# GpSimd sums the derived token quarters from quarters that DMA has turned; the next x is prepared one step earlier

## The chip, the cores and the metric

One core of one Trainium2 chip. The metric is device time per execution in microseconds (us); lower is better. Three runs of the kernel before gave a median of 3518.05 us (3515.58 to 3518.43).

## The reference

The input x has 8 x 1024 tokens of 512 features. The kernel computes `x + s * g`, where `xn = layernorm(x)`, `s` is an attention block of 16 heads on `xn`, and `g = silu(spikes(y) / 5)` with

```python
h = square(relu(xn @ W_fc.T))        # 512 -> 2048
y = h @ W_proj.T                     # 2048 -> 512
# five steps of a leaky integrator count how often it passes its threshold
```

The change concerns how `xn @ W_fc.T` gets its moving operands. The kernel does that product by a Strassen-like scheme: a block of 512 tokens by 512 features is cut into quarters (two halves of the tokens by two halves of the features), and seven products of quarters or of sums of quarters take the place of eight. Every operand is split into a high and a low f16 part, and three of the four partial products are kept.

## The kernel before, in words

The first stage is the feed-forward block, on 16 chunks (`NC` = 16, `c` = 0 to 15) of 512 tokens. A chunk has 8 steps (`PAIRS` = 8, `p` = 0 to 7, `n = 8c + p`). In a step TensorE does the seven products of one slice of 256 hidden features (`product(n, 0)` to `product(n, 6)`, six matmuls each, L727), and between them eight groups of projection matmuls for the hidden slices of earlier steps (`proj`, L744). The second stage, attention, begins at about 1376 us; only its first group of heads is prepared inside the last two chunks.

All engines run a fixed order that is written out by hand (`step` in each engine's block); semaphores keep them together. In each step:

- ACT copies partial sums out of PSUM (`snapshot` 0 to 2, L982, and `take_sum`, L988) and makes the high parts of the hidden slices (`hid_hi`, L975). `after_first` to `after_fourth` are the places for other work; `after_fourth` comes behind `take_sum`. ACT also issues the load of the next weights (L890).
- VectorE adds the partial sums (`combine(n, 0)` to `combine(n, 2)`, L1335; product 3 waits for `combine` 0, product 6 for `combine` 1, product 1 of the next step for `combine` 2), squares (`square`, L1320) and makes low parts (`hid_lo`, L1327). In steps 2 to 5 it counts the spikes of the chunk before (`count`, L168 and L171), in steps 4, 6 and 7 it makes gate tiles (`gate_tile`, L178).
- GpSimd multiplies each gate tile by gamma and adds beta's part to x (`multiply`, L123, L125, L127: three instructions for each of four tiles).

While chunk c runs, chunk c + 1 is prepared. For c of 1 or more: VectorE takes statistics of x in step 0 (`statistics`, L1229; `variances`), normalises in step 1 (L1261), ACT and VectorE split into high and low f16 in steps 2 and 3 (`part_hi`, L925; `part_lo`, L1277). SP then issues 32 DMAs that turn 128x128 pieces of it (`turn`, L496: two parts, four tiles of tokens, four blocks of features) into `xnT`: these are the natural quarters, with the features on the partitions. For chunk 1, in chunk 0, all this is one step later.

The four derived quarters are made apart from that. GpSimd forms them on the unturned `xn` (`make_turns`, L587 to L592, four instructions of 128x512), into the memory in which x had stood; ACT and VectorE split them (`turned_hi`, L931, in steps 3 and 4; `turned_lo`, L1281, in steps 4 and 5); TensorE turns them through PSUM (`turn_quarter`, L638, four groups of eight matmuls in two steps named by `TURN_AT`, steps 5 and 6); ACT copies them out (`copy_turned`, L941) into `xnS`. When the derived quarters have been split, ACT issues the load of the following x (`fetch_x`, L946). For chunk 0 other functions do this.

SP's queue within chunk c: store `xnT` of chunk c to memory, load x again for the output (`load_base`), copy rows of a table, issue the 32 turns for chunk c + 1, and at last, when GpSimd has done the twelve multiplications of chunk c - 1, store gate and base (L160).

## Time and profile before

| | us |
|---|---|
| median of three runs | 3518.05 |
| the profiled execution | 3518.49 |
| its span, first to last instruction | 3516.7 |
| TensorE busy | 3384.6 |
| VectorE busy | 2804.3 |
| ACT busy | 2779.1 |
| GpSimd busy | 1862.4 |
| feed-forward stage, 27.5 to about 1376 | 1349 |
| a regular chunk of it (531.23 to 612.29) | 81.06 |

PE is TensorE, DVE is VectorE, POOL is GpSimd, SP the engine that issues most DMAs. Busy times are unions over the span; `x` counts instructions. PEclk is the granted TensorE clock as a share of 2.4 GHz. A chunk's times below are counted from its first product, steps from their own.

### The profile page before, as it was taken

The page shows a single profiled execution, that of the slowest core. Times are in us where ns is not written, and L with a number is a line of the kernel's source. Part 1 is how long each engine was busy: PE and PEld are TensorE (multiplying, and loading weights), DVE is VectorE, ACT ScalarE, POOL GpSimd, SP SyncE. Part 2 cuts the span into 40 slices and gives each one's busy share as a digit, 9 for nine tenths or more (in the row PEclk, how much of TensorE's full clock was granted, in tenths as well). Part 3 has the DMA queues.
Part 4 walks back from the last instruction along what each step waited for, and adds up shares of the span by engine and source line. Part 5 has one row for each costly group of instructions (what it writes and reads, how often), then busy time and mean ns, then how long its engine had stood idle before and what let it go on. Part 6 is the DMA issues. An engine that isn't in the chain of part 4 may idle for free.

```text
span 3516.7 us, 63651 instructions
## 1 busy us (share of the span) xinstructions
PE 3384.6 (96%) x22764; PEld 1693.4 (48%) x22764; DVE 2804.3 (80%) x4812; ACT 2779.1 (79%) x4531; POOL 1862.4 (53%) x1094
## 2 busy tenths in 40 slices
PE   6999999999999999999999999999999999999996
PEld 4666666666666665334334334433433433433432
DVE  7878887777877866777788788788788888888887
ACT  6555444444444455999999999999999999999996
POOL 4223332223222314998756766766766766666662
PEclk9999999999999999999999999999999999999998
DMA  5655555555555543222332232232332322322322
GB/s 204 210 165 177 196 173 180 189 190 176 168 176 175 166 150 119 72 67 82 112 100 79 88 94 81 92 94 81 92 94 80 93 91 82 94 88 82 98 61 85
DMA packets 257226, 430.34 MB, mean 122 GB/s; under 512 B 98672, under 2 KB 134256, under 8 KB 256912
## 3 DMA queue, kind: packets, MB, share of 16 engines
q1 hardware_dynamic: 231088, 294.13, 27.1%
q10 hardware_dynamic: 25824, 132.13, 10.8%
q8 instruction: 183, 3.00, 0.4%
q14 instruction: 131, 1.07, 0.1%
HBM read 284.75 MB, written 83.95 MB: 105 GB/s over the span
## 4 chain that ended last, share of the span: by engine, by line
ACT 32%; PE 13%; issue 10%; DVE 4%; SPq 1%; DMA 1%; ACTq 0%; DVEq 0%
ACT recurrence_or_probs L1903 17%; ACT s_sb L1910 15%; PE misc L1777 3%; PE acc L1852 3%; PE s_ps L1832 3%; PE s_ps L1818 3%; DVE s_sb L1979 2%; SPq L320 1%; DMA xT<-xnT 1%; DVE gate_or_tokens L2108 1%; PE misc L1759 0%; DVE x_or_queries L2016 0%; DVE outT L1999 0%; DVE gate_or_tokens L2111 0%; PE s_ps L1777 0%
## 5 line engine op out<-in xcount | busy, mean ns | idle before, releaser
L1979 DVE TENSOR_SCALAR_CACHE_REDUCE s_sb<-s_ps 128x1024 f32<-128x1024 f32 x998 | 1214.4, 1221 | 354.4 <-PE s_ps L1818 326.3
L2185 POOL TENSOR_TENSOR recurrence_or_probs<-recurrence_or_probs,toep 128x512 f32<-128x512 f32 (+1 forms) x375 | 1288.9, 3458 | 365.9 <-ACT recurrence_or_probs L1903 365.5
L1910 ACT ACTIVATE s_sb<-s_sb,nmax 128x1024 f32<-128x1024 f32 x998 | 1166.3, 1169 | 9.7 <-DVE s_sb L1979 9.2
L1903 ACT ACTIVATE recurrence_or_probs<-s_ps 128x1024 f32<-128x1024 f32 x1024 | 1060.5, 1037 | 9.5 <-PE s_ps L1832 9.3
L744 PE MATMUL ps_y<-w_pr,hid_part 128*128 128x512 f16 x3072 | 807.6, 379 | 0.0
L1852 PE MATMUL acc<-recurrence_or_probs,val 128*32 128x512 f32 x4096 | 546.6, 606 | 2.2 <-DVE recurrence_or_probs L2095 1.5
L982 ACT ACTIVATE snap<-ps_fc 128x256 f32<-128x256 f32 x384 | 147.5, 384 | 468.7 <-PE ps_fc L727 453.7
L123 POOL TENSOR_TENSOR recurrence_or_probs<-gate_or_tokens,gamma_beta 128x512 f32<-128x512 f32 x60 | 86.0, 1434 | 595.5 <-DVE gate_or_tokens L178 594.4
L744 PEld LDWEIGHTS ps_y<-w_pr,hid_part 128*128 128x128 f16 x3072 | 300.5, 98 | 173.4
L727 PE MATMUL ps_fc<-xnT_part,w_fc 128*128 128x256 f16 x2304 | 314.8, 273 | 17.8 <-DVE u L1335 11.6
L1818 PE MATMUL s_ps<-kst,qst 96*128 96x512 f16 x1024 | 306.0, 380 | 25.5 <-ACT recurrence_or_probs L1903 25.4
L1832 PE MATMUL s_ps<-x_or_queries 99*128 99x512 f16 x1024 | 307.5, 381 | 5.3 <-DVE s_sb L1979 5.2
L1832 PE MATMUL s_ps<-qst,kst 99*128 99x512 f16 x1024 | 307.7, 383 | 1.7 <-DVE s_sb L1979 1.6
L1818 PE MATMUL s_ps<-x_or_queries 96*128 96x512 f16 x972 | 290.3, 379 | 15.8 <-ACT recurrence_or_probs L1903 15.8
L727 PEld LDWEIGHTS ps_fc<-xnT_part,w_fc 128*128 128x128 f16 x2304 | 222.2, 98 | 124.3 <-DVE u L1335 20.3
L1320 DVE SCALAR_TENSOR_TENSOR hid<-u 128x512 f32<-128x512 f32 x256 | 202.5, 791 | 97.7 <-ACT u L988 49.1
L1335 DVE TENSOR_TENSOR u<-ps_fc,snap 128x256 f32<-128x256 f32 x384 | 161.2, 420 | 143.4 <-PE ps_fc L727 77.3
L1327 DVE TENSOR_TENSOR hid_part<-hid,hid_part 128x512 f16<-128x512 f32 x256 | 238.3, 934 | 11.9 <-ACT hid_part L975 11.8
L1910 ACT ACTIVATION_READ_ACCUMULATOR s_sb<-s_sb,nmax 128x1 f32 x998 | 219.4, 220 | 0.0
L727 PE MATMUL ps_fc<-xnS_part,w_fc 128*128 128x256 f16 x1536 | 210.2, 273 | 9.1 <-DVE u L1335 6.8
L727 PE MATMUL ps_fc<-recurrence_or_probs,w_fc 128*128 128x256 f16 x1536 | 209.6, 273 | 3.8 <-DVE u L1335 3.0
L171 DVE SCALAR_TENSOR_TENSOR recurrence_or_probs<-recurrence_or_probs 128x512 f32<-128x512 f32 x240 | 190.8, 795 | 0.6
(206 smaller groups left out, 4076.9 us busy)
## 6 DMA issues: line engine op xcount, KB each, us to landing
w_fc<-fc_made ACTq DMA_DIRECT2D x120, 896.0 KB, 5.0
toep<-table_rows SPq DMA_DIRECT2D x32, 2048.0 KB, 8.3
x_or_queries<-x_or_queries SPq DMA_DIRECT2D x384, 64.0 KB, 2.0
xnT<-xnT_part SPq DMA_DIRECT2D x32, 512.0 KB, 11.3
x_or_gate<-in_x SPq DMA_DIRECT2D x16, 1024.0 KB, 9.1
...
```

The lines of the kernel that those rows point to most:

```text
L171: op = self.nc.vector.scalar_tensor_tensor(spikes, y, self.thresholds[i], spikes, ALU.is_ge, ALU.add)
L727: last = nc.tensor.matmul(bank, w["fc"][:, n % RINGW, i, a, k, :], moving, start=(m == 0 and i in (0, 1, 3)), stop=(m == 5), skip_group_ch ...
L744: last = nc.tensor.matmul(ps_y[:, t, :], hid_part[:, f % 4, a, t * P:(t + 1) * P], w["pr"][:, b, f, :], start=(f == 0 and m == 0), stop=(f ...
L1320: nc.vector.scalar_tensor_tensor(hid[:, f, :], u[:, f, :], 0.0, u[:, f, :], ALU.max, ALU.mult).then_inc(sq_done, 1)
L1327: nc.vector.tensor_tensor(hid_part[:, f % 4, 1, :], hid[:, f % 2, :], hid_part[:, f % 4, 0, :], ALU.subtract).then_inc(lo_done, 1)
L1818: last = nc.tensor.matmul(s_ps[:, item_buffer(x), c * 512:(c + 1) * 512], qst[par][0:ROWS, j, st * P:(st + 1) * P], kst[par][0:ROWS, j, c ...
L1832: last = nc.tensor.matmul(s_ps[:, item_buffer(x), i * 512:(i + 1) * 512], kst[s.par][:ROWS + SUBTRACTED, j, tb * P:(tb + 1) * P], qst[s.pa ...
L1852: last = nc.tensor.matmul(acc[j * HD:(j + 1) * HD, :], val[:, par, tb, j * HD:(j + 1) * HD], prob[:, k % PROBS, j, :], start=(tb == 0), st ...
L1903: nc.scalar.activation(prob[:, k % PROBS, 2 * second:2 * second + 2, :].rearrange("p j n -> p (j n)"), s_ps[:, item_buffer(pair_item(m)), ...
L1910: nc.scalar.activation(s_sb[:, i % 4, :], s_sb[:, i % 4, :], ACT.Exp, bias=nmax[:, par, j, st:st + 1], scale=-1.0, accum_out=den[:, par, j ...
L1979: nc.vector.tensor_scalar(s_sb[:, i % 4, :], s_ps[:, item_buffer(tile_item(n)), :], -1.0, None, ALU.mult, ALU.min, accum_out=nmax[:, par, ...
L2185: nc.gpsimd.tensor_tensor(tile, tile, toep[:, par, :, at:at + width], ALU.add).then_inc(biased, 1)
```

## The change

For chunks 2 to 15, GpSimd makes the derived quarters from the turned natural quarters: `join_quarter` adds the high and the low part of a natural quarter in `xnT` (f16) into `xn` (f32, whose normalised values are no longer needed then), and `turned_sum` forms a difference or sum of two of these. ACT and VectorE split the results straight into `xnS` (`turned_hi`, `turned_lo`). `make_turns`, `turn_quarter` and `copy_turned` remain for chunk 1 alone (and chunk 0 as before). SP issues the 32 turns by quarters, in the order of need, each quarter after both of its parts are split, and counts each quarter on a semaphore of its own. The splitting of the derived quarters stands in steps 5, 6 and 7 of a chunk (6 and 7 in chunk 1). The preparation of x (`prepared`) begins in step 7 of the chunk before from chunk 3's x on, one step sooner; the load of x moves from ACT to SP, ahead of the turns. In steps 23, 30 and 31 the four `qkv_lo` are spread otherwise over the step.

```diff
@@ -207,15 +207,15 @@
-TURN_AT = {c * 8 + 5 + (c == 0) + h: (c + 1, 2 * h) for c in range(15) for h in range(2)}
+TURN_AT = {6: (1, 0), 7: (1, 2)}
...
-TURNS_AT = ({4: (0, 1), 5: (2, 3)}, {3: (0, 1), 4: (2, 3)})
-TURNS_LO_AT = ({5: (0, 1), 6: (2, 3)}, {4: (0, 1), 5: (2, 3)})
+TURNS_AT = ({4: (0, 1), 5: (2, 3)}, {6: (0, 1), 7: (2, 3)}, {5: (0,), 6: (1, 2), 7: (3,)})
+TURNS_LO_AT = ({5: (0, 1), 6: (2, 3)}, {6: (0, 1), 7: (2, 3)}, {5: (0,), 6: (1, 2), 7: (3,)})
...
@@ -468,6 +469,27 @@
+        def prepared(n, k):
+            n -= k
+            if n == 1:
+                return 1
+            if n == PAIRS:
+                return 2
+            c = (n + 1) // PAIRS + 1
+            return c if n > PAIRS and n % PAIRS == PAIRS - 1 and c < NC else None
+        def wait_turned(eng, c):
+            if c > 0:
+                for q in range(4):
+                    eng.wait_ge(xt_turned[q], c * TURNED)
+        def natural(par, part, q):
+            k, half = ((2, HALF), (0, 0), (0, HALF), (2, 0))[q]
+            return xnT[:, par, part, k:k + 2, half:half + HALF]
...
@@ -489,12 +511,14 @@
-                for part, done in ((0, xn_hi), (1, xn_lo)):
-                    for t in range(4):
-                        sp.wait_ge(done, (c - 1) * 4 + t + 1)
-                        for k in range(EB):
-                            sp.dma_start(xnT[:, par, part, k, t * P:(t + 1) * P], xn_part[:, part, t, k * P:(k + 1) * P],
-                                         transpose=True).then_inc(xt_turned, 16)
+                for q, tokens_half, k_half in ((2, 1, 0), (0, 1, 1), (1, 0, 0), (3, 0, 1)):
+                    sp.wait_ge(xn_hi, c * 4 - 2 + 2 * tokens_half)
+                    sp.wait_ge(xn_lo, c * 4 - 2 + 2 * tokens_half)
+                    for part in range(2):
+                        for t in (2 * tokens_half, 2 * tokens_half + 1):
+                            for k in (2 * k_half, 2 * k_half + 1):
+                                sp.dma_start(xnT[:, par, part, k, t * P:(t + 1) * P], xn_part[:, part, t, k * P:(k + 1) * P],
+                                             transpose=True).then_inc(xt_turned[q], 16)
...
@@ -531,6 +555,9 @@
+                if 0 < c < NC - 2:
+                    sp.wait_ge(xn_ready, c * 4 + 8)
+                    load_x(c + 2)
...
@@ -542,8 +569,9 @@
-                    sp.wait_ge(xt_turned, (NC - 1) * TURNED)
-                    sp.wait_ge(xs_ps, NC * 4)
+                    wait_turned(sp, NC - 1)
+                    sp.wait_ge(turn_hi, (NC - 1) * 4)
+                    sp.wait_ge(turn_lo, (NC - 1) * 4)
...
@@ -590,6 +618,20 @@
+            def join_quarter(c, q, done):
+                if done == 0:
+                    pool.wait_ge(xn_hi, c * 4)
+                    pool.wait_ge(xn_lo, c * 4)
+                pool.wait_ge(xt_turned[q], c * TURNED)
+                nc.gpsimd.tensor_tensor(xn[:, q, :].rearrange("p (k s) -> p k s", k=2), natural(c % 2, 0, q), natural(c % 2, 1, q),
+                                        ALU.add).then_inc(sum_made, 1)
+            def turned_sum(c, q, a, b, op, done):
+                pool.wait_ge(sum_made, (c - 2) * 8 + done)
+                nc.gpsimd.tensor_tensor(xn[:, q, :], xn[:, a, :], xn[:, b, :], op).then_inc(sum_made, 1)
...
@@ -606,17 +648,25 @@
-            for c in range(1, NC):
-                if c < NC - 1:
-                    make_turns(c + 1)
-                else:
-                    pool.wait_ge(xt_turned, (NC - 1) * TURNED)
-                    nc.gpsimd.memset(first.kst[ROWS:ROWS + SUBTRACTED], 1.0).then_inc(first.ones_set, 1)
-                    pool.wait_ge(first.ones_set, 1)
-                for t in range(4):
+            for c in range(1, NC - 1):
+                join_quarter(c + 1, 2, 0)
+                join_quarter(c + 1, 0, 1)
+                turned_sum(c + 1, 0, 0, 2, ALU.subtract, 2)
+                spiking.multiply(c - 1, 0)
+                join_quarter(c + 1, 1, 3)
+                turned_sum(c + 1, 2, 2, 1, ALU.subtract, 4)
+                turned_sum(c + 1, 1, 0, 1, ALU.add, 5)
+                join_quarter(c + 1, 3, 6)
+                turned_sum(c + 1, 3, 3, 1, ALU.subtract, 7)
+                for t in range(1, 4):
...
-                    if c == NC - 1 and t == 0:
-                        first.subtracted(pool, 0, 0, 0)
+            wait_turned(pool, NC - 1)
+            nc.gpsimd.memset(first.kst[ROWS:ROWS + SUBTRACTED], 1.0).then_inc(first.ones_set, 1)
+            pool.wait_ge(first.ones_set, 1)
+            for t in range(4):
+                spiking.multiply(NC - 2, t)
+                if t == 0:
+                    first.subtracted(pool, 0, 0, 0)
...
@@ -716,6 +766,10 @@
+                if n > PAIRS and p == 0 and i in (2, 3, 4, 6):
+                    made = (c - 1) * 4 + {2: 2, 3: 2, 4: 3, 6: 4}[i]
+                    pe.wait_ge(turn_hi, made)
+                    pe.wait_ge(turn_lo, made)
...
@@ -921,14 +975,20 @@
-                    wait(act, xt_turned, (c - 1) * TURNED)
+                    wait_turned(act, c - 1)
...
-                if j == 0:
-                    act.wait_ge(turns_made, c * 4 + 4)
-                    act.wait_ge(xn_lo, c * 4)
-                nc.scalar.activation(turn_part[:, 0, j], turns[:, j], ACT.Copy).then_inc(turn_hi, 1)
+                if c == 1:
+                    if j == 0:
+                        act.wait_ge(turns_made, c * 4 + 4)
+                        act.wait_ge(xn_lo, c * 4)
+                    nc.scalar.activation(turn_part[:, 0, j], turns[:, j], ACT.Copy).then_inc(turn_hi, 1)
+                else:
+                    if j == 0:
+                        act.wait_ge(multiplied, (c - 1) * PAIRS * PRODUCTS)
+                    act.wait_ge(sum_made, (c - 2) * 8 + (3, 6, 6, 8)[j])
+                    nc.scalar.activation(xnS[c % 2][:, 0, j].rearrange("p k s -> p (k s)"), xn[:, j, :], ACT.Copy).then_inc(turn_hi, 1)
...
@@ -1074,8 +1125,8 @@
-                if c < NC - 1 and p in TURNS_AT[c > 0]:
-                    for j in TURNS_AT[c > 0][p]:
+                if c < NC - 1 and p in TURNS_AT[min(c, 2)]:
+                    for j in TURNS_AT[min(c, 2)][p]:
...
@@ -1257,7 +1308,11 @@
-                    wait(dve, xs_ps, c * 4)
+                    if c <= 2:
+                        wait(dve, xs_ps, c * 4)
+                    else:
+                        dve.wait_ge(turn_hi, (c - 1) * 4)
+                        dve.wait_ge(turn_lo, (c - 1) * 4)
...
@@ -1273,12 +1328,16 @@
-                    wait(dve, xt_turned, (c - 1) * TURNED)
+                    wait_turned(dve, c - 1)
...
-                nc.vector.tensor_tensor(turn_part[:, 1, j], turns[:, j], turn_part[:, 0, j], ALU.subtract).then_inc(turn_lo, 1)
+                if c == 1:
+                    nc.vector.tensor_tensor(turn_part[:, 1, j], turns[:, j], turn_part[:, 0, j], ALU.subtract).then_inc(turn_lo, 1)
+                else:
+                    hi, lo = (xnS[c % 2][:, part, j].rearrange("p k s -> p (k s)") for part in range(2))
+                    nc.vector.tensor_tensor(lo, xn[:, j, :], hi, ALU.subtract).then_inc(turn_lo, 1)
...
@@ -1344,14 +1403,15 @@
-                ahead, late = c < NC - 1, c == 0
+                ahead = c < NC - 1
+                begun, refined, split = prepared(n, 0), prepared(n, 1), (prepared(n, 2), prepared(n, 3))
...
-                if ahead and p == 0 + late:
-                    statistics(c + 1, 0)
+                if begun:
+                    statistics(begun, 0)
...
-                if ahead and p == 3 + late:
-                    part_lo(c + 1, 2)
+                if split[1]:
+                    part_lo(split[1], 2)
...
@@ -1360,45 +1420,48 @@
-                if ahead and p == 0 + late:
+                if n in QKV_LO_AT:
+                    qkv_lo(QKV_LO_AT[n], 0)
+                if begun:
...
-                        statistics(c + 1, t)
-                if ahead and p == 1 + late:
-                    refine(c + 1)
-                    normalise(c + 1, 0)
-                    normalise(c + 1, 1)
+                        statistics(begun, t)
+                if refined:
+                    refine(refined)
+                    normalise(refined, 0)
+                    normalise(refined, 1)
...
-                if ahead and p == 2 + late:
-                    part_lo(c + 1, 0)
-                if ahead and p == 3 + late:
-                    part_lo(c + 1, 3)
+                if split[0]:
+                    part_lo(split[0], 0)
+                if split[1]:
+                    part_lo(split[1], 3)
...
-                    for k in range(3):
-                        qkv_lo(QKV_LO_AT[n], k)
+                    qkv_lo(QKV_LO_AT[n], 1)
...
+                if n in QKV_LO_AT:
+                    qkv_lo(QKV_LO_AT[n], 2)
...
-                if ahead and p == 1 + late:
-                    normalise(c + 1, 2)
+                if refined:
+                    normalise(refined, 2)
...
-                if ahead and p == 0 + late:
-                    variances(c + 1)
+                if begun:
+                    variances(begun)
...
-                if ahead and p == 1 + late:
-                    normalise(c + 1, 3)
+                if refined:
+                    normalise(refined, 3)
...
-                if ahead and p == 2 + late:
-                    part_lo(c + 1, 1)
-                if ahead and p in TURNS_LO_AT[c > 0]:
-                    for j in TURNS_LO_AT[c > 0][p]:
+                if split[0]:
+                    part_lo(split[0], 1)
+                if ahead and p in TURNS_LO_AT[min(c, 2)]:
+                    for j in TURNS_LO_AT[min(c, 2)][p]:
...
...
```

## Rows read from the trace of the kernel before

**Rows 1.** Page, part 1: busy us, share of the span, instructions, by engine.

```profile
PE 3384.6 (96%) x22764; PEld 1693.4 (48%) x22764; DVE 2804.3 (80%) x4812; ACT 2779.1 (79%) x4531; POOL 1862.4 (53%) x1094
```

**Rows 2.** Windows of chunk 6, whole and steps 2, 4, 5, 6: stretch, length, then busy us.

```profile
531.23:612.29 81.06, 80.25 (x561) 53.29 (x560) 63.78 (x106) 38.37 (x82) 24.02 (x16) 1.00 0.53 177
...
550.76:560.52 9.76, 9.76 (x67) 6.45 (x66) 9.74 (x14) 4.76 (x10) 3.78 (x3) 1.00 0.35 109
...
570.28:580.31 10.03, 9.93 (x67) 6.38 (x66) 8.89 (x12) 5.28 (x11) 4.75 (x3) 1.00 0.41 116
...
580.31:591.85 11.54, 10.84 (x83) 7.27 (x82) 10.03 (x18) 6.20 (x13) 0.00 (x0) 1.00 0.36 105
...
591.85:602.51 10.66, 10.66 (x83) 7.35 (x82) 5.82 (x10) 6.19 (x13) 6.40 (x5) 1.00 0.60 198
```

**Rows 3.** Timeline of TensorE, step 3 of chunk 6: start, duration, instructions merged.

```profile
560.53 0.71 PE L727 MATMUL ps_fc<-xnT_part,w_fc 128*128 128x256 f16 x5
...
568.99 0.82 PE L727 MATMUL ps_fc<-xnS_part,w_fc 128*128 128x256 f16 x6
...
571.60 0.27 PE L727 MATMUL ps_fc<-xnT_part,w_fc 128*128 128x256 f16 x1
```

**Rows 4.** Timeline of TensorE, step 5 of chunk 6, with the wait before it.

```profile
582.50 0.83 PE L727 MATMUL ps_fc<-xnT_part,w_fc 128*128 128x256 f16 x6 [0.70 <-DVE u L1335]
...
583.82 0.61 PE L638 MATMUL ps_t<-identh,x_or_queries 128*128 128x128 f16 x8
...
584.26 0.27 PE L727 MATMUL ps_fc<-xnS_part,w_fc 128*128 128x256 f16 x1
```

**Rows 5.** Instructions of line 638, the turning matmuls, in the whole span.

```profile
L638 PE MATMUL ps_t<-identh,x_or_queries x480: 219/219/230, 98.4 to 1254.1; 128*128 128x128 f16 x160
```

**Rows 6.** Timeline of GpSimd, chunk 6: two of make_turns, the last multiplication.

```profile
548.57 1.27 POOL L587 TENSOR_TENSOR x_or_queries<-x_or_queries 128x512 f32<-128x512 f32 x1 [19.21 <-DVE x_or_queries L1261]
...
551.47 1.73 POOL L590 TENSOR_TENSOR x_or_queries<-x_or_queries 128x512 f32<-128x512 f32 x1
...
608.82 1.60 POOL L127 TENSOR_TENSOR gate_or_tokens<-gate_or_tokens,gamma_beta 128x512 f32<-128x512 f32 x1
```

**Rows 7.** VectorE in chunk 6: line 1327's times (ns, min/median/max), then its timeline.

```profile
L1327 DVE TENSOR_TENSOR hid_part<-hid,hid_part x16: 675/683/1754, 533.7 to 607.5; 128x512 f16<-128x512 f32 x16
...
551.99 1.50 DVE L168 TENSOR_SCALAR recurrence_or_probs<-recurrence_or_probs 128x512 f32<-128x512 f32 x1
...
559.03 0.68 DVE L1277 TENSOR_TENSOR x_or_queries<-x_or_queries 128x512 f16<-128x512 f32 x1
...
559.63 0.68 DVE L1320 SCALAR_TENSOR_TENSOR hid<-u 128x512 f32<-128x512 f32 x1
...
602.67 1.31 DVE L1320 SCALAR_TENSOR_TENSOR hid<-u 128x512 f32<-128x512 f32 x1
...
603.90 1.76 DVE L178 SCALAR_TENSOR_TENSOR gate_or_tokens<-recurrence_or_probs,gate_or_tokens 128x512 f32<-128x512 f32 x1
...
605.58 0.41 DVE L1335 TENSOR_TENSOR u<-ps_fc,snap 128x256 f32<-128x256 f32 x1
...
605.91 3.38 DVE L1327 TENSOR_TENSOR hid_part<-hid,hid_part 128x512 f16<-128x512 f32 x2
```

**Rows 8.** SP in chunk 6: the 32 turns in its timeline; all turns' time to landing.

```profile
553.29 43.61 SPq L496 DMA_TRANSPOSE xnT_part<-x_or_queries  x32
...
DMA to landing us min/median/max: 2.2/3.1/7.7
```

**Rows 9.** Timelines around chunk 1's start: SP's turns, VectorE's last split, TensorE.

```profile
65.66 45.84 SPq L496 DMA_TRANSPOSE xnT_part<-x_or_queries  x32
...
81.83 0.68 DVE L1277 TENSOR_TENSOR x_or_queries<-x_or_queries 128x512 f16<-128x512 f32 x1
...
117.12 0.82 PE L727 MATMUL ps_fc<-xnT_part,w_fc 128*128 128x256 f16 x6
```

**Rows 10.** Window behind the first product: busy us, then granted clock (PEclk).

```profile
27.46:40.00 12.54, 10.33 (x63) 6.22 (x64) 7.07 (x14) 9.82 (x14) 3.96 (x6) 0.86 0.78 288
```

**Rows 11.** Timeline of ACT, end of step 4 of chunk 6: two turned_hi.

```profile
578.59 1.14 ACT L931 ACTIVATE x_or_queries<-x_or_queries 128x512 f16<-128x512 f32 x2
```

42 lines of the change are left out of this document (17 added, 25 removed).

## The prediction

> **What bounds the kernel now.** I read the page first: TensorE is busy for 96% of the span [rows 1]. The attention stage (from about 1376 us on) is not touched by the change, so I read the feed-forward stage alone, by chunks. The windows of one regular chunk (531.23 to 612.29, number 6 of 0 to 15, one of ten alike, chunks 4 to 13) show TensorE busy for 80.25 of 81.06 us [rows 2]. The steps of it show where it is not full: an unstalled step takes 9.76 us, step 4 takes 10.03, step 5 takes 11.54, step 6 takes 10.66 and step 7 the rest, 9.78. So a chunk is 8 x 9.76 = 78.1 plus 2.95 us. The timeline of TensorE tells what the 2.95 are [rows 4]: four groups of eight turning matmuls, each of 584.26 - 583.82 = 0.44 us, 1.78 together; and waits for VectorE (L1335, the `combine`) of 2.95 - 1.78 = 1.17 us, of which the largest stands before 582.50.
>
> So TensorE bounds a regular chunk, and VectorE is a close second. Why it is late in steps 4 and 5 is seen by laying the GpSimd rows [rows 6] beside the VectorE rows [rows 7]. A subtraction of two SBUF tensors (L1327) takes 0.68 us, and 1.75 while GpSimd runs (two in 3.38 us from 605.91); the square (L1320) takes 1.31 instead of 0.68; the gate 1.76 instead of 0.68. A `combine`, which reads PSUM, stays at 0.41. GpSimd's multiplications stretch to 1.6 us too. GpSimd is idle most of a chunk (24.0 of 81 us busy, and its share by step stands in [rows 2]), so this price is paid today in few steps.
>
> When VectorE is late enough to cost something follows from a regular step of TensorE [rows 3]: product 6 starts 568.99 - 560.53 = 8.46 us into the step and needs `combine` 1; product 1 of the next step starts 11.07 us after the step's start and needs `combine` 2. Everything that VectorE finishes later than that stops TensorE.
>
> **The change, part by part.**
>
> *Turning gone.* 480 turning matmuls are 15 chunks of 32 [rows 5]; chunks 2 to 15 lose theirs, 14 x 1.78 = 24.9 us, all on the path. ACT loses eight copies per chunk; it is not the bound, worth nothing. If the 1.17 us of waits went as well in 14 chunks, 16 us more.
>
> *GpSimd.* Per chunk four `make_turns` (5.9 us, steps 1 and 2, where VectorE has room) go, and eight instructions come: four `join_quarter` and four `turned_sum`. The sums have the shape of [rows 6]. For a join of two f16 inputs there is no row: below, 1.27 us (the fp32 sum undisturbed), above, 1.73 with some conversion on top; I take 1.5, since VectorE will be busy beside it. The Trainium skill (GPSIMD Engine Reference, 3.1 Elementwise — side-by-side cycle accounting) gives about 2.6 cycles per element for two inputs and so 4497 ns for 2048 elements; by that the join would be about 1.1 us (an estimate), four of them 1.6 us less, and the sum below some 10 us lower. No run here shows which.
>
> *When the joins can run.* They wait for the DMA turns, which SP issues one after another: 32 in 43.61 us, landing 3.1 us (median) after issue, up to 7.7 [rows 8]. Today the first goes as soon as the first tile is split; in the new order it waits for all eight halves, the last of which is `part_lo` 3, now in step 2. `part_lo` is 0.68 us (559.03 in [rows 7]); its place in step 2 puts it at about 24 us from the chunk's start. At 43.61 / 4 = 10.9 us for eight turns, and two or three more for the last landing, the quarters are there at about 36, 47, 57 and 68 us. SP reaches the turns in time: after GpSimd's last multiplication it needs some 10 us for its stores and loads, the moved load of x (one issue) included. x then has four steps until step 7: hidden.
>
> GpSimd's queue, in its order: join at 36; join, difference 47 to 50; the previous chunk's `multiply` of tile 0 (three instructions) 50 to 55; join and two sums 57 to 61; join and sum 68 to 71; nine multiplications 71 to 86. From 47 to 86 it is busy for about 31 of 39 us, and that is exactly steps 5 to 7.
>
> *VectorE in steps 5 to 7.* `turned_lo` moves there (one, two, one), the statistics of the next x move into step 7 (2.4 us and 0.8 of aggregates). I lay the instructions out with the two prices of [rows 7], an instruction starting about 0.08 before the end of the last one as there.
> Step 5 (starts 48.8): square 1.3, first count 1.5, `combine` 0 at 52.1, subtraction 1.7, count 1.5, then count, subtraction free, count 1.6; `combine` 1 ends at 58.5, wanted at 57.3: 1.2 late. Count 1.7, `turned_lo` 1.5, square 0.7; `combine` 2 ends at 62.6, wanted at 61.1: 1.5 late. With undisturbed GpSimd times (1.3 each) it is 1.6 instead of 2.7.
> Step 6: GpSimd is quiet until the last quarter lands. But `turned_lo` now stands behind `turned_hi` of the same step, which ACT starts 8.3 us into it (578.59 in [rows 11], in the step from 570.28). Two of them at 1.75 under GpSimd, the square at 1.3: `combine` 2 ends 13.9 us into the step, wanted at 11.07: 2.8 late.
> Step 7: square, one statistic, gate (1.76), `combine` 0: 1.3 late; two subtractions at 1.7, three statistics, `combine` 1: 0.3 to 0.9 more. Then GpSimd ends, and step 0 is free. I take the statistics (one input) as undisturbed; no row of this stage shows them beside GpSimd, and at most they would cost as the two-input ones do, 1.07 each.
> If the third quarter lands a microsecond later, step 5 loses less and step 7, nearer to the multiplications, as much more. Sum: 6.1 to 7.9 us, I take 7.0. A chunk is then 78.1 + 7.0 = 85.1 against 81.06: +4.05, ten regular chunks +40.5.
>
> *Chunk 1* still prepares one step late, so its quarters land 10 us later (46, 57, 66, 78) while `turned_hi` for two quarters is due at the end of step 6 (67): the sums are there at about 72, ACT and with it VectorE stand for 5 us, step 7 adds 3: 86.6 against 81.07, +5.5. *Chunks 2 and 3* also carry the splitting of the attention weights in steps 6 and 7, and chunk 2 the rest of GpSimd's late work: +5 each. *Chunk 14* has 10 us of attention matmuls in steps 5 to 7, which give VectorE room: turning gone, waits come, 0 (bounds -3, +4).
>
> *The start of chunk 1.* The new issue order has its price once. Today the 32 turns for chunk 1 are issued from 65.66 to 111.50, and TensorE, which waits for the landing of all of them, begins the chunk at 117.12 [rows 9]. In the new order none starts before the last `part_lo`, at 82.5 (81.83 + 0.68). 82.6 plus 42 to 46 plus a landing is 127 to 131: TensorE stands still for 10 to 14 us, I take 12. The clock may fall as well: in the 12.54 us behind the start of the first product, before which TensorE had waited, the granted clock was 0.86, so a part of them at 1.2 instead of 2.4 GHz [rows 10]; that is (1 - 0.86) x 12.54 = 1.8 us of work, which I count inside the 10 to 14.
>
> *The rest* (the split of `qkv_lo` within its step, the new waits of SP, TensorE and DVE before the attention stage) is under work that is there anyway: 0; without that cover below 1 us each.
>
> Sum against the profiled execution (3518.49, 0.44 above the median of the runs): 12 + 5.5 + 10 + 40.5 + 0 = +68, 3586 us. The removed 24.9 us are inside the chunk differences.
>
> **Rivals.**
> A, faster: *TensorE stays the bound.* VectorE's added time fits into its slack (it is busy 63.8 of 81 us), or the joins disturb it less than fp32 sums do. What decides is `combine` 1 of step 5: done by 57.3, nothing is lost there. Then -24.9, waits between today's and none (0 to -16), +12 at chunk 1: 3489 to 3506. For: on average there is room. Against: the price is plain where both engines run, the sixteen L1327 of chunk 6 go from 0.675 to 1.754 us [rows 7], and the joins stand in three steps in a row. Chance 0.17.
> B: *it pays back what it saves.* Half of my waits come: 3.5 us per chunk in place of 2.95, so +0.5 in 13 chunks, +12, and the weights' chunks: 3526 to 3548. For: GpSimd may be less disturbed than taken. Chance 0.14; a fourth of it so low that it can't be told from no change.
> C: *the sums come too late everywhere.* If the DMA turns slip by 6 us or more (landing took up to 7.7), ACT stands before `turned_hi` in step 6 of each chunk, as it does in chunk 1. +9 in 14 chunks and 12: 3656. Against: 5.7 us of slack in step 6. Chance 0.08.
>
> **How the numbers follow.** My case has 0.61, from 3548 to 3620. About 0.2% (7 us) is what a measurement of this kernel tells from no change. Faster: A, 0.17. Same: 0.04, out of B. Slower: 0.79. The range leaves out C and the lower half of A: 3498 to 3622.
>
> **What would show it.** Right: steps 5, 6 and 7 of a regular chunk take over 11 us each with TensorE waiting for L1335; `turned_lo` at 1.75 us; GpSimd busy from 47 to 86 us of the chunk; one TensorE gap of 10 us or more near 117 us. Wrong: regular chunks of 78 to 80 us, or joins beside which VectorE keeps 0.68. Wrong in size: the quarters landing elsewhere than at 36, 47, 57 and 68.

## The result, and the profile after

The kernel after takes 3577.22 us (median of four runs, 3562.65 to 3580.01) against 3516.89 (four runs, 3515.58 to 3518.43) beside it: ratio 1.0157, interval 1.0124 to 1.0189. It is slower, by 60 us where the prediction said 68.

The page of the kernel after, the engines' busy times (us, share of the span of 3577.8 us, instructions):

```profile
PE 3384.0 (95%) x22316; PEld 1673.5 (47%) x22316; DVE 2848.3 (80%) x4812; ACT 2724.2 (76%) x4419; POOL 1943.6 (54%) x1150
```

TensorE has 448 matmuls fewer and is busy as long as before [rows 1], in a span 61.1 us longer. Two things hide in that: its waits, and matmuls that run at the lower of its two clock levels. To find where the 61 us lie I took the starts of the first product of each step from the trace; the differences are the lengths of chunks and steps.

| chunk | before | after | difference |
|---|---|---|---|
| 0 (to the first product of chunk 1) | 89.66 | 101.33 | +11.67 |
| 1 | 81.07 | 87.02 | +5.95 |
| 2 | 85.90 | 96.45 | +10.55 |
| 3 | 85.01 | 91.25 | +6.24 |
| 4 to 13, ten regular ones | 810.7 | 838.7 | +28.0 |
| 14 | 91.99 | 90.07 | -1.92 |
| 15 (to the end of its last product) | 95.06 | 95.07 | 0 |

They add up to 60.5; what follows chunk 15 is the same to 0.5 us.

**The start of chunk 1.** The timeline of TensorE in the kernel after, then its windows around the gap (length, busy us of PE, PEld, DVE, ACT, POOL, then PEclk, DMA share, GB/s):

```profile
116.79 0.59 PE L798 MATMUL ps_y<-w_pr,hid_part 128*128 128x512 f16 x2
128.88 1.44 PE L781 MATMUL ps_fc<-xnT_part,w_fc 128*128 128x256 f16 x6 [11.49 <-DMA xnT_part<-x_or_queries]
```

```profile
117.00:128.80 11.80, 0.38 (x2) 0.00 (x0) 1.49 (x3) 0.00 (x0) 0.00 (x0) 0.64 0.13 25
128.80:141.00 12.20, 12.12 (x66) 7.34 (x67) 6.65 (x17) 3.91 (x8) 0.00 (x0) 0.79 1.01 350
```

TensorE stands still for 11.49 us until the turned quarters have landed. Then six matmuls take 1.44 us instead of 0.82 [rows 9]: the granted clock is 0.79 in the next 12.2 us, so a part of them runs at 1.2 instead of 2.4 GHz, and step 0 of chunk 1 is 12.24 us long instead of 9.76.

**A regular chunk.** Chunk 6 is now 574.16 to 658.16. Its steps 4 to 7 and the whole, in the windows of the kernel after (columns as above):

```profile
613.47:623.23 9.76, 9.76 (x67) 6.44 (x66) 7.26 (x13) 4.24 (x9) 2.14 (x2) 1.00 0.40 118
623.23:632.99 9.76, 9.76 (x67) 6.47 (x66) 9.53 (x11) 4.76 (x10) 6.05 (x5) 1.00 0.39 120
632.99:644.38 11.39, 9.94 (x67) 6.38 (x66) 8.15 (x12) 5.28 (x11) 5.34 (x5) 1.00 0.35 103
644.38:658.16 13.78, 11.63 (x68) 7.02 (x66) 13.20 (x20) 3.20 (x7) 13.22 (x9) 0.88 0.20 67
574.16:658.16 84.00, 80.32 (x530) 52.05 (x528) 65.63 (x107) 34.36 (x74) 27.91 (x20) 0.98 0.52 171
```

Against [rows 2]: step 5, the longest before, is free; step 7 takes 13.78 us, with VectorE and GpSimd both busy nearly all of it. TensorE's busy time there is 11.63 us where the same matmuls take 9.76 in step 5, at a granted clock of 0.88. So the loss in step 7 is waiting and also clock.

TensorE's waits in the same chunk (timeline of TensorE, kernel after):

```profile
635.93 0.83 PE L781 MATMUL ps_fc<-xnT_part,w_fc 128*128 128x256 f16 x6 [1.45 <-DVE u L1394]
...
648.01 0.83 PE L781 MATMUL ps_fc<-xnT_part,w_fc 128*128 128x256 f16 x6 [2.15 <-DVE u L1394]
...
649.33 1.44 PE L781 MATMUL ps_fc<-xnS_part,w_fc 128*128 128x256 f16 x6
...
660.76 0.83 PE L781 MATMUL ps_fc<-xnT_part,w_fc 128*128 128x256 f16 x6 [1.14 <-DVE u L1394]
```

The three waits stand before product 1 of a step (6, 7, and 0 of the next chunk), which needs `combine` 2 (L1394 now) of the step before. The row at 649.33 shows the clock: 1.44 us for six matmuls, soon after the longest of the waits.

What stands ahead of the `combine` is in the timelines of VectorE and of GpSimd in the kernel after:

```profile
643.59 2.37 DVE L1340 TENSOR_TENSOR recurrence_or_probs<-x_or_queries,recurrence_or_probs 128x512 f16<-128x512 f32 x2 [1.97 <-ACT recurrence_or_probs L991]
645.88 1.75 DVE L1379 SCALAR_TENSOR_TENSOR hid<-u 128x512 f32<-128x512 f32 x1
647.54 0.41 DVE L1394 TENSOR_TENSOR u<-ps_fc,snap 128x256 f32<-128x256 f32 x1
...
649.22 0.68 DVE L1280 BATCH_NORM_STATS2 stats<-x_or_queries 128x6 f32<-128x512 f32 x1
```

```profile
611.21 1.15 POOL L628 TENSOR_TENSOR x_or_queries<-xnT_part 128x512 f32<-128x512 f16 x1 [37.04 <-DMA xnT_part<-x_or_queries]
621.01 1.15 POOL L628 TENSOR_TENSOR x_or_queries<-xnT_part 128x512 f32<-128x512 f16 x1 [8.65 <-DMA xnT_part<-x_or_queries]
...
627.01 1.60 POOL L127 TENSOR_TENSOR gate_or_tokens<-gate_or_tokens,gamma_beta 128x512 f32<-128x512 f32 x1
632.16 1.16 POOL L628 TENSOR_TENSOR x_or_queries<-xnT_part 128x512 f32<-128x512 f16 x1 [3.55 <-DMA xnT_part<-x_or_queries]
633.39 3.27 POOL L634 TENSOR_TENSOR x_or_queries<-x_or_queries 128x512 f32<-128x512 f32 x2
642.48 1.16 POOL L628 TENSOR_TENSOR x_or_queries<-xnT_part 128x512 f32<-128x512 f16 x1 [5.82 <-DMA xnT_part<-x_or_queries]
...
658.23 1.59 POOL L127 TENSOR_TENSOR gate_or_tokens<-gate_or_tokens,gamma_beta 128x512 f32<-128x512 f32 x1
```

The joins (L628) start when their quarters have landed, 37.1, 46.9, 58.0 and 68.3 us into the chunk; GpSimd ends at 85.7. VectorE stands 1.97 us for ACT's `turned_hi`, then has two `turned_lo` (2.37 us together) and a square of 1.75 us before its `combine`.

Over the ten regular chunks the waits view (engine, line, what it waits for: us, times, longest) has for the kernel after, 403 to 1242 us:

```profile
PE ps_fc L781 <- DVE u L1394: 39.6, 35, 3.3
```

and for the kernel before, 369 to 1180 us:

```profile
PE ps_fc L727 <- DVE u L1335: 7.1, 10, 0.7
```

The ten chunks of the kernel after take 57.9 us more than 10 x 78.08. The view's 39.6 are waits; the lower clock is 10.2 (1.7 in each of six chunks, see the last section); the remaining 8 us show in neither.

**Where the waits are, kernel by kernel.** The table gives what each step takes beyond the unstalled 9.76 us, as the mean of the ten regular chunks 4 to 13 (from the products' starts), for the experiments too. A wait for `combine` 2 counts in the step behind it; time lost to the lower clock counts where it is lost. Steps 1 to 3 take 9.76 in all of them. Each row is one execution. Before the change the ten chunks are alike (81.06 and 81.07); after it they are not (80.16 to 85.76, in e1 79.54 to 90.24), so a few tenths between two rows mean nothing.

| kernel | step 0 | 4 | 5 | 6 | 7 | chunk |
|---|---|---|---|---|---|---|
| before | 0 | 0.28 | 1.78 | 0.90 | 0 | 81.07 |
| after | 1.25 | 0 | 0.26 | 1.11 | 3.16 | 83.87 |
| e1_old_turn_order | 0.79 | 0 | 0.20 | 1.41 | 3.56 | 84.07 |
| e2_small_multiplies | 0 | 0 | 0.27 | 1.17 | 1.41 | 80.96 |
| e3_small_gpsimd | 0 | 0 | 0 | 0 | 0.23 | 78.35 |
| e4_lo_behind_combine | 0.60 | 0 | 0.20 | 0.34 | 2.99 | 82.23 |
| e5_prepared_late | 1.80 | 0 | 0 | 5.09 | 0.50 | 85.50 |
| e6_small_joins | 0.93 | 0 | 0 | 0 | 1.16 | 80.20 |
| e7_before_gates_late | 0 | 0 | 0.90 | 0.90 | 0 | 79.91 |
| e8_reordered | 0.73 | 0 | 0.24 | 1.80 | 0.20 | 81.07 |

### The profile page after: what moved, and what is told of

Read it like the earlier page. It is cut to its first block, busy times and chain, and to the rows that moved or that the text cites. A ratio compares the mean times of both kernels' runs of the same rounds, so it can differ in the third digit from the quotient of the medians.

```text
span 3577.8 us, 62836 instructions
## 1 busy us (share of the span) xinstructions
PE 3384.0 (95%) x22316; PEld 1673.5 (47%) x22316; DVE 2848.3 (80%) x4812; ACT 2724.2 (76%) x4419; POOL 1943.6 (54%) x1150
## 4 chain that ended last, share of the span: by engine, by line
ACT 31%; PE 13%; issue 10%; DVE 3%; DMA 1%; SPq 1%; ACTq 0%; DVEq 0%
ACT recurrence_or_probs L1966 16%; ACT s_sb L1973 15%; PE misc L1840 3%; PE acc L1915 3%; PE s_ps L1895 3%; PE s_ps L1881 3%; DVE s_sb L2042 2%; DMA xT<-xnT 1%; SPq L320 1%; PE misc L1822 1%; DVE gate_or_tokens L2171 0%; DVE outT L2062 0%; DVE x_or_queries L2079 0%; DVE gate_or_tokens L2174 0%; PE s_ps L1840 0%
## 5 line engine op out<-in xcount | busy, mean ns | idle before, releaser
L798 PE MATMUL ps_y<-w_pr,hid_part 128*128 128x512 f16 x3072 | 817.2, 382 | 0.0
L628 POOL TENSOR_TENSOR x_or_queries<-xnT_part 128x512 f32<-128x512 f16 x56 | 71.3, 1274 | 794.7 <-DMA xnT_part<-x_or_queries 794.7
L1379 DVE SCALAR_TENSOR_TENSOR hid<-u 128x512 f32<-128x512 f32 x256 | 245.6, 959 | 71.8 <-issue 57.5
L1394 DVE TENSOR_TENSOR u<-ps_fc,snap 128x256 f32<-128x256 f32 x384 | 161.2, 420 | 158.0 <-PE ps_fc L781 85.6
L1386 DVE TENSOR_TENSOR hid_part<-hid,hid_part 128x512 f16<-128x512 f32 x256 | 215.3, 841 | 10.1 <-ACT hid_part L1035 9.9
L1035 ACT ACTIVATE hid_part<-hid 128x512 f16<-128x512 f32 x256 | 160.3, 626 | 50.4 <-DVE hid L1379 44.5
```

Of the source, the lines that this page charges most:

```text
L798: last = nc.tensor.matmul(ps_y[:, t, :], hid_part[:, f % 4, a, t * P:(t + 1) * P], w["pr"][:, b, f, :], start=(f == 0 and m == 0), stop=(f ...
L1379: nc.vector.scalar_tensor_tensor(hid[:, f, :], u[:, f, :], 0.0, u[:, f, :], ALU.max, ALU.mult).then_inc(sq_done, 1)
L1386: nc.vector.tensor_tensor(hid_part[:, f % 4, 1, :], hid[:, f % 2, :], hid_part[:, f % 4, 0, :], ALU.subtract).then_inc(lo_done, 1)
L1394: nc.vector.tensor_tensor(out, bank, snap[:, m, :], ALU.add).then_inc(combined, 1)
```

## The experiments

The theory (theory 1 in the expectations) is that of the prediction: GpSimd's work now lies in the steps in which VectorE must also make `turned_lo`, each slows the other, and VectorE comes late. The kernels of e2, e3 and e6 leave out a part of GpSimd's work and don't compute the whole result. The first four runs share ten runs of the kernel before (median 3516.24), the last four twelve (3517.97).

### e1: the turns of chunk 1 in the old order

```diff
             def turn(c):
...
+                if c == 1:
+                    for part, done in ((0, xn_hi), (1, xn_lo)):
+                        for t in range(4):
+                            sp.wait_ge(done, t + 1)
+                            for k in range(EB):
+                                sp.dma_start(xnT[:, par, part, k, t * P:(t + 1) * P], xn_part[:, part, t, k * P:(k + 1) * P],
+                                             transpose=True).then_inc(xt_turned[((1, 3), (2, 0))[t // 2][k // 2]], 16)
+                    return
```

> The changed kernel with one thing undone: for chunk 1 alone, SP issues the 32 turns as the kernel before does, by part and tile, each as soon as its tile is split; they still count on the four quarters' semaphores. Theory 1 (the new issue order makes TensorE wait once at the start of chunk 1, because no turn may start before the last split): the TensorE gap of 11.5 us in front of chunk 1 goes, chunk 1 starts at about 117.1 us, nothing else changes: 10 to 13 us less than the changed kernel, about 3566 us. Rival (the gap only takes up lateness that comes anyway, since the sums for chunk 2 are late in chunk 1): the gap goes, but chunk 1 gets longer by about as much: within 3 us of the changed kernel.

Measured: 3562.34 us (3555.29 to 3569.25), ratio 1.0133 (1.0117 to 1.0150). SP's timeline of this kernel, then that of the kernel after:

```profile
64.99 47.02 SPq L519 DMA_TRANSPOSE xnT_part<-x_or_queries  x32
```

```profile
82.68 44.85 SPq L520 DMA_TRANSPOSE xnT_part<-x_or_queries  x32
```

The turns start 17.7 us sooner, chunk 1 at 116.46 instead of 128.88 us, and its step 0 takes 9.77 us. The longer chunk 1 that the rival foresaw doesn't come (84.38 us against 87.02). The intervals of the two ratios overlap, but the trace leaves no doubt about the gap: it is gone, with the clock loss behind it. The new order of issue, which needs all eight halves first, costs 12.4 us of waiting and 2.5 of clock, once; the prediction said 10 to 14 with the clock in it.

### e2: three of the four multiplications small

```diff
+        n = 512 if t == 0 or c == 14 else 32
-        pool, gate, product, done = self.nc.gpsimd, self.gate[:, t, :], self.product[:, t, :], (c * 4 + t) * 3
+        pool, gate, product, done = self.nc.gpsimd, self.gate[:, t, :n], self.product[:, t, :n], (c * 4 + t) * 3
...
-        self.nc.gpsimd.tensor_tensor(gate, gate, self.gamma, ALU.mult).then_inc(self.multiplied, 1)
+        self.nc.gpsimd.tensor_tensor(gate, gate, self.gamma[:, :n], ALU.mult).then_inc(self.multiplied, 1)
```

> The changed kernel, but three of the four gate multiplications of a chunk (tiles 1 to 3, in all chunks but the last) treat 32 of 512 columns; the other 480 columns of these tiles are left out, waits and order stay. GpSimd is then idle in step 7 and at the start of the next step 0, while joins, sums and every wait for them stay. Theory 1 (VectorE loses to GpSimd at the shared memory access): step 7 of a regular chunk falls from about 13 to under 11.5 us and step 0 from 11 to under 10.2: 25 to 50 us less than the changed kernel, about 3540 us. Rival (VectorE is late because turned_lo waits behind ACT and behind late sums): the multiplications cost nothing, steps 6 and 7 stay, within 8 us of the changed kernel.

Measured: 3527.47 us (3523.06 to 3528.85), ratio 1.0032 (1.0021 to 1.0044), 50 less than after. Step 7 loses 1.41 us instead of 3.16, step 0 nothing; chunk 2 falls from 96.45 to 84.11, chunk 3 from 91.25 to 82.90. Steps 5 and 6 don't change, as they shouldn't: in them GpSimd still has its joins, its sums and tile 0.

### e3: GpSimd's added work and its multiplications small

The edit of e2 for all four tiles (`n = 512 if c == 14 else 32`), and in `join_quarter` and `turned_sum`:

```diff
-                nc.gpsimd.tensor_tensor(xn[:, q, :].rearrange("p (k s) -> p k s", k=2), natural(c % 2, 0, q), natural(c % 2, 1, q),
+                nc.gpsimd.tensor_tensor(xn[:, q, :].rearrange("p (k s) -> p k s", k=2)[:, :, :16], natural(c % 2, 0, q)[:, :, :16], natural(c % 2, 1, q)[:, :, :16],
...
-                nc.gpsimd.tensor_tensor(xn[:, q, :], xn[:, a, :], xn[:, b, :], op).then_inc(sum_made, 1)
+                nc.gpsimd.tensor_tensor(xn[:, q, :32], xn[:, a, :32], xn[:, b, :32], op).then_inc(sum_made, 1)
```

> As the run with small multiplications, and all four multiplications, the joins and the sums treat 32 of 512 columns (a sixteenth of each is done, the rest left out; the last chunk's multiplications whole). The DMA turns and every wait stay, GpSimd hardly works in chunks 1 to 13. Theory 1: regular chunks fall to 78.1 plus at most 1 us, with chunk 1's start wait still there: about 3505 us (3495 to 3520), so below the kernel before. Rival (late sums, VectorE waiting behind ACT): step 6 and step 7 keep 1 to 2 us each, regular chunks of 81 to 82: about 3545 us.

Measured: 3490.69 us (3489.34 to 3491.38), ratio 0.9929 (0.9914 to 0.9944), below the 3495 to 3520 that I expected. The window of its chunk 6:

```profile
529.66:608.07 78.41, 78.30 (x530) 51.60 (x528) 54.63 (x107) 34.35 (x74) 8.26 (x20) 1.00 0.56 186
```

TensorE is busy for 78.30 of 78.41 us. The order of the instructions, the DMA turns and the late landings are as in the kernel after, only GpSimd's durations are not: VectorE's busy time falls by 11.0 us (65.63 to 54.63) with the same instructions, and the waits are gone. With the gap at chunk 1 still in it this kernel is 26 us faster than before: 24.9 of turning and 14 x 1.17 of old waits, less the 14 us at chunk 1, would be 27. So the loss comes from GpSimd's durations; late landing and order alone cost 0.23 us a chunk.

Shorter instructions on GpSimd also finish its sums sooner, so a rival is left: that ACT's `turned_hi` waited for late sums. The kernel after itself answers it. The view of its `turned_hi` (L991) lists what ACT stood idle for ahead of these 56 instructions (us, times) in the whole run, and has one row:

```profile
  POOL x_or_queries L634: 4.7, 1
```

The one wait for a sum is in step 7 of chunk 1 (at 203.56). In the regular chunks no sum was late; what GpSimd costs there is the longer time of VectorE's instructions.

### e4: `turned_lo` behind `combine` 2

```diff
-                if ahead and p in TURNS_LO_AT[min(c, 2)]:
-                    for j in TURNS_LO_AT[min(c, 2)][p]:
-                        turned_lo(c + 1, j)
...
                 square(2 * n)
...
                 combine(n, 2)
+                if ahead and p in TURNS_LO_AT[min(c, 2)]:
+                    for j in TURNS_LO_AT[min(c, 2)][p]:
+                        turned_lo(c + 1, j)
```

> The changed kernel with turned_lo moved behind combine 2 in VectorE's step, so that the square and combine 2 no longer stand behind ACT's turned_hi. Theory 1 (VectorE has too much to do in steps 5 to 7 while GpSimd works): the lateness moves from step 6 into the start of step 7, where turned_lo now stands before the square: 15 us less to 15 us more than the changed kernel. Rival (the order is what costs, VectorE stands idle behind ACT): steps 6 and 7 lose 1.5 us each and step 0 one: about 35 us less, 3542 us.

Measured: 3554.79 us (3551.52 to 3559.01), ratio 1.0113 (1.0098 to 1.0128), 22 less than after. That is below theory 1's range (3562 to 3592) and above the rival's 3542. VectorE's timeline in its chunk 6, around the start of step 7:

```profile
635.38 2.24 DVE L1340 TENSOR_TENSOR recurrence_or_probs<-x_or_queries,recurrence_or_probs 128x512 f16<-128x512 f32 x2
637.55 1.75 DVE L1379 SCALAR_TENSOR_TENSOR hid<-u 128x512 f32<-128x512 f32 x1
639.22 0.68 DVE L1280 BATCH_NORM_STATS2 stats<-x_or_queries 128x6 f32<-128x512 f32 x1
639.83 1.14 DVE L178 SCALAR_TENSOR_TENSOR gate_or_tokens<-recurrence_or_probs,gate_or_tokens 128x512 f32<-128x512 f32 x1
640.89 0.41 DVE L1394 TENSOR_TENSOR u<-ps_fc,snap 128x256 f32<-128x256 f32 x1
```

The wait for ACT in front of `turned_lo` is gone and step 6 loses 0.34 us instead of 1.11. But the same 2.24 and 1.75 us then stand ahead of step 7's `combine` 0 (640.89), and step 7 keeps 2.99 of its 3.16. The order is a part of the cost, 1.6 us a chunk; the rest moves with the work.

### e5: x prepared at the old place

```diff
-            if n == PAIRS:
-                return 2
-            c = (n + 1) // PAIRS + 1
-            return c if n > PAIRS and n % PAIRS == PAIRS - 1 and c < NC else None
+            c = n // PAIRS + 1
+            return c if n >= PAIRS and n % PAIRS == 0 and c < NC else None
```

> The changed kernel with the earlier preparation undone: statistics of the next x again in step 0, normalising in step 1, splitting in steps 2 and 3. Theory 1 (GpSimd and VectorE collide in steps 5 to 7): the DMA turns start and the quarters land about 10 us later, so that the sums are late for turned_hi in steps 5 to 7, and the nine multiplications run in steps 0 and 1 of the next chunk; each regular chunk gets 2 to 6 us longer: about 3620 us (3595 to 3660). Rival (the collision with the statistics in step 7 is what costs): step 7 gets lighter by 3 us and the kernel faster: 3540 to 3570 us.

Measured: 3592.48 us (3584.57 to 3595.66), ratio 1.0206 (1.0191 to 1.0222), 15 more than after. VectorE's waits for `turned_hi` on ACT in the regular chunks, by the waits view of this kernel (390 to 1230 us) and then of the kernel after (403 to 1242):

```profile
DVE xnS_part L1338 <- ACT xnS_part L989: 43.7, 14, 4.7
DVE recurrence_or_probs L1338 <- ACT recurrence_or_probs L989: 43.7, 15, 7.8
```

```profile
DVE recurrence_or_probs L1340 <- ACT recurrence_or_probs L991: 11.6, 9, 2.0
DVE xnS_part L1340 <- ACT xnS_part L991: 10.7, 7, 2.0
```

The two tiles are those of even and odd chunks. ACT in turn waits for GpSimd's sums; its view of `turned_hi` (L989) has, beside 2.2 us for TensorE:

```profile
  POOL x_or_queries L632: 44.7, 24
```

This is rival C, made to happen. The sums are late for step 6, and it loses 5.09 us. It costs less than expected, since step 7 loses only 0.50. Two things have left that step: the statistics, and most of GpSimd's work (it is busy for 3.65 us in step 7 of chunk 6, 644.18 to 655.18, against 13.22 in the kernel after); which of the two counts isn't shown. Step 7 thus gets lighter by 2.7 us, as this run's rival had it, but the kernel gets slower. So the earlier preparation is worth 15 us to the new scheme by the medians, just below the range that I had put on it; the two executions behind the table (3584.57 and 3579.67) are 5 us apart.

### e6: joins and sums small, multiplications whole

The second half of e3's edit alone.

> The changed kernel with joins and sums on 32 of 512 columns (the rest left out), the multiplications whole. Theory 1: only what GpSimd's eight new instructions take from VectorE goes; the multiplications start 3 us sooner and stay in steps 6 and 7, so step 5 and 6 lose their waits, step 7 most of its own stays: 10 to 25 us less than the changed kernel, about 3560 us. Rival (the new instructions are the whole cost): all waits but the order's go, about 3525 us, as in the run with small multiplications or below.

Measured: 3528.27 us (3526.69 to 3531.62), ratio 1.0030 (1.0018 to 1.0041), 49 less than after. Here the rival's number came and theory 1's did not. The rival's reason did not come: the chunks take 80.20 us against 78.35 in e3, so the multiplications alone still cost something. The price is not with the multiplications, as I had concluded from e2: taking away either group removes most of the loss, 50 and 49 us, both together 86. With small joins steps 5 and 6 lose nothing, product 1 of step 7 starts only 0.3 us late on the mean (1.9 in the kernel after), and the multiplications alone then cost 2.1 us (steps 7 and 0). With small multiplications steps 5 and 6 lose their 1.4 us and step 7 another 1.4. I read this so: what VectorE comes late by into step 7 it lacks for the work that waits there. No run varies that lateness alone.

### e7: the kernel before, its first gate two steps later

```diff
-GATES_AT = ({4: (0,), 5: (1,), 6: (2,)}, {4: (0,), 6: (1, 2)})
+GATES_AT = ({4: (0,), 5: (1,), 6: (2,)}, {6: (0, 1, 2)})
```

> The kernel BEFORE with one line changed: the first gate tile, so far in step 4, is made in step 6 with the second and third. GpSimd's first multiplication then runs in step 6, not in steps 4 and 5 beside VectorE's counts. Theory 1 (a VectorE that has too much to do for as long as GpSimd works is what stops TensorE): the 0.28 us of step 4 and the 0.87 us of step 5 go, steps 6 and 7 have the room: 1.17 us in each of 12 or 13 chunks, 3502 us. Rival (the wait in steps 4 and 5 is turned_lo's own): nothing changes, or step 7 gets longer by as much: 3514 to 3522 us.

Measured: 3507.04 us (3505.09 to 3510.01), ratio 0.9968 (0.9956 to 0.9980). Its chunk 6 in the windows, steps 4, 5 and 6 and the whole:

```profile
571.30:581.06 9.76, 9.76 (x67) 6.46 (x66) 7.73 (x15) 5.29 (x11) 0.00 (x0) 1.00 0.40 116
581.06:591.96 10.90, 10.90 (x84) 7.45 (x83) 8.21 (x15) 6.20 (x13) 0.00 (x0) 1.00 0.38 111
591.96:602.60 10.64, 10.64 (x83) 7.35 (x82) 7.86 (x9) 6.21 (x13) 6.37 (x5) 1.00 0.64 202
...
532.48:612.39 79.91, 79.91 (x562) 53.43 (x560) 63.90 (x108) 38.44 (x82) 24.36 (x17) 1.00 0.55 179
```

In the kernel before, the gate tile in step 4 let GpSimd multiply beside VectorE in that step, from 574.85 to 579.76; in step 5 it did nothing [rows 2]. Timelines of GpSimd and of VectorE there, in the kernel before:

```profile
574.85 1.56 POOL L123 TENSOR_TENSOR recurrence_or_probs<-gate_or_tokens,gamma_beta 128x512 f32<-128x512 f32 x1 [20.23 <-DVE gate_or_tokens L178]
```

```profile
575.20 1.75 DVE L1327 TENSOR_TENSOR hid_part<-hid,hid_part 128x512 f16<-128x512 f32 x1
```

So the larger wait, in step 5, came from lateness that VectorE brought along out of step 4. With the gate in step 6 GpSimd has 0.00 us in step 4, VectorE is busy for 7.73 us there instead of 8.89 and for 8.21 in step 5 instead of 10.03 (the gate's own 0.69 us is in the difference), and TensorE is busy all of the chunk. The 1.17 us of waits per chunk that the prediction left to VectorE are gone, and what is over 8 x 9.76 is the turning alone: 1.8 us, as costed. Chunks 2 and 3 pay 1.6 and 3.6 us of it back. One line thus gives 11 us, and of all versions that compute the whole result this is the fastest.

### e8: the change, put in a better order

e1's edit; the statistics in step 6; ACT's `turned_hi` of step 6 at `after_second`, with VectorE's `turned_lo` before `combine` 1; `turned_lo` of steps 5 and 7 behind `combine` 2:

```diff
+                if c >= 2 and p == 6 and c < NC - 1 and p in TURNS_AT[min(c, 2)]:
+                    for j in TURNS_AT[min(c, 2)][p]:
+                        turned_hi(c + 1, j)
...
-                begun, refined, split = prepared(n, 0), prepared(n, 1), (prepared(n, 2), prepared(n, 3))
+                begun = prepared(n, -1) if (prepared(n, -1) or 0) > 2 else None if (prepared(n, 0) or 0) > 2 else prepared(n, 0)
+                refined, split = prepared(n, 1), (prepared(n, 2), prepared(n, 3))
+                if c >= 2 and p == 6 and ahead and p in TURNS_LO_AT[min(c, 2)]:
+                    for j in TURNS_LO_AT[min(c, 2)][p]:
+                        turned_lo(c + 1, j)
```

> The changed kernel with three moves together: turns for chunk 1 in the old order; statistics of the next x (from chunk 3's on) in step 6 in place of step 7; in step 6 turned_hi behind ACT's second snapshot and turned_lo in front of combine 1, in steps 5 and 7 turned_lo behind combine 2. Theory 1: VectorE works where it stood idle (the 2 us behind combine 1 of step 6), but GpSimd still takes as much from it: regular chunks of 80 to 82 us, 3515 to 3535 us, so not below the kernel before by more than 0.2%. Rival (order and idle places were the whole price): regular chunks below 79.5, about 3495 us.

Measured: 3534.49 us (3530.84 to 3538.18), ratio 1.0045 (1.0030 to 1.0060), 43 less than after. A regular chunk takes 81.07 us on average, exactly as before: the turning saved is paid back in waits, as in rival B. What is over is chunks 1 to 3 (83.31, 93.49 and 92.02 us, together +16.8). Chunk 3 loses 8.64 us beyond 9.76 in step 6, where a split of the attention weights and now the statistics stand. Chunk 2 loses 9.56 in step 0 (1.73 in the kernel before), where no `qkv_lo` stands but nine of GpSimd's multiplications run late; so the weights are not the whole of it. No version of the change that computes the whole result beat the kernel before.

## Why the prediction was right

The direction, the mechanism and the size came: GpSimd lengthens VectorE's instructions in the steps in which both work, and TensorE waits for `combine`. Term by term:

**Turning gone, 24.9 us.** Right: e7 shows two steps of 0.90 us each where only turning is over, and e3 the chunk of 78.35 us that is left when nothing waits.

**The start of chunk 1, 10 to 14, I took 12.** The gap is 11.7 and the clock adds 2.5 (12.24 against 9.76 in step 0): 14.2, just above the upper end. I had counted 1.8 for the clock inside the range and not on top of my 12.

**When the joins can run.** I had 36, 47, 57 and 68 us, measured 37.1, 46.9, 58.0 and 68.3; GpSimd busy from 47 to 86, measured 46.9 to 85.7.

**The join, taken at 1.5 us.** It takes 1.15 to 1.16 us in the rows above and 1.27 on the mean of 56 (71.3 us in all). The estimate of 1.1 us from the Trainium skill (GPSIMD Engine Reference, 3.1 Elementwise — side-by-side cycle accounting) was nearer than mine, and it agrees with the undisturbed join, though its figure is for f32 inputs and the undisturbed f32 sum takes 1.27 us [rows 6]. The forecast from that sentence, some 10 us lower, would have been 3576, closer to the 3577 measured, though not for this reason alone.

**A regular chunk, 85.1.** It takes 83.87: 5.8 us beyond 78.1 instead of 7.0. Term by term, by the waits of chunk 6: `combine` 1 of step 5, 1.2 late: not there. The third quarter landed 1 us later than I had it, GpSimd stood idle for 3.55 us before it, and VectorE caught up, which is the case that the prediction names. `combine` 2 of step 5, 1.5 late: 1.45. `combine` 2 of step 6, 2.8 late: 2.15. `combine` 0 and 1 of step 7, together 1.6 to 2.2: nothing here; 0.5 to 0.6 in the five chunks (4, 8, 9, 11, 13) whose step 7 kept the full clock. Step 0, free: a wait of 1.14. And the clock, in no term of a regular chunk: 1.65 us in step 7, (1 - 0.88) x 13.78. Chunk 6 is one of ten that differ. On their mean, by how much later than in an unstalled step each product starts:

| what TensorE waited for | predicted | chunk 6 | mean of ten |
|---|---|---|---|
| `combine` 1 of step 5 | 1.2 | 0 | 0.24 |
| `combine` 2 of step 5 | 1.5 | 1.6 | 1.09 |
| `combine` 2 of step 6 | 2.8 | 2.3 | 1.89 |
| `combine` 0 and 1 of step 7, and the clock there | 1.6 to 2.2 | 1.7 | 1.27 |
| step 0 | 0 | 0.3 | 1.25 |

The last row is the chunk's own step 0, after the chunk before it; the wait of 1.14 falls in chunk 7. So the sum was good to a fifth, in part by luck: on the mean each of its four terms was too large, and step 0 and the clock were left out. Its bounds of 6.1 to 7.9 don't come out of its terms either: these give 7.1 to 7.7, or from 6.0 on with the undisturbed times in step 5.

**Chunk 1, +5.5:** +5.95, of which 2.5 are the clock at its start. ACT stood 4.7 us for the sum, as predicted (5). Of the 3 us more in step 7 only 1.5 came, and those are the lower clock; VectorE's part came as 4.5 us more in step 0 of chunk 2. And 78.1 + 5 + 3 is 86.1, not the 86.6 of the prediction. That the number came so close is luck. **Chunks 2 and 3, +5 each:** +10.55 and +6.24, the term that was most too small. Step 0 of chunk 2 has 4.5 us of it (6.27 beyond 9.76 against 1.73 before), with the multiplications that chunk 1 left over; step 7 has 7.8 and takes 19.22 us. VectorE's timeline there in the kernel after, with `qkv_lo` (L1233), and TensorE's:

```profile
301.30 1.75 DVE L1233 SCALAR_TENSOR_TENSOR w_q<-gate_or_tokens,work,w_q 128x512 f16<-128x512 f32 x1
...
304.76 1.31 DVE L1233 SCALAR_TENSOR_TENSOR w_q<-gate_or_tokens,work,w_q 128x512 f16<-128x512 f32 x1
306.00 1.75 DVE L1386 TENSOR_TENSOR hid_part<-hid,hid_part 128x512 f16<-128x512 f32 x1
307.67 1.75 DVE L1233 SCALAR_TENSOR_TENSOR w_q<-gate_or_tokens,work,w_q 128x512 f16<-128x512 f32 x1
309.34 0.41 DVE L1394 TENSOR_TENSOR u<-ps_fc,snap 128x256 f32<-128x256 f32 x1
```

```profile
296.74 0.83 PE L781 MATMUL ps_fc<-xnT_part,w_fc 128*128 128x256 f16 x6 [2.15 <-DVE u L1394]
...
309.81 1.46 PE L781 MATMUL ps_fc<-xnS_part,w_fc 128*128 128x256 f16 x6 [4.06 <-DVE u L1394]
```

Three of the weights' splits, at 1.3 to 1.75 us, stand in the queue ahead of `combine` 1, beside two subtractions and three statistics, and `combine` 1 releases product 6 after 4.06 us. I had given these chunks a round +5 without laying out their queue.

**Chunk 14, -3 to +4:** -1.9. **The statistics beside GpSimd, undisturbed:** right, 0.68 us at 649.22 while GpSimd multiplies.

**The square, 1.31 under GpSimd:** the first square of a step took 1.75 at 645.88.

**The signs.** The gap near 117 us and GpSimd's busy time from 47 to 86 us came as named. Of steps 5, 6 and 7, named at over 11 us each, only step 7 is (12.92 on the mean; step 5 10.02, step 6 10.87), and `turned_lo` took anything from 0.68 to 1.81 us.

**Rivals.** A's point of decision, `combine` 1 of step 5, was on time in chunk 6 and late by 0.24 on the mean, and the time was lost all the same, at `combine` 2: the point was badly chosen. B is what e8 shows once the order is mended. C is e5.

The parts of my cost that lay too high (the four waits of a regular chunk) and those too low (chunks 2 and 3, the clock, step 0) cancel to 8 us: the ten regular chunks cost 28.0 us instead of 40.5, chunks 2 and 3 16.8 instead of 10. The direction and the mechanism are shown by e3; the share of each piece of GpSimd's work is not a fixed number, as e2 and e6 show.
